# Four graph layers in one kernel: scaling and degree work moved to GpSimd, score halves side by side, loads two groups ahead, tables of their own for both ends, stores from ScalarE

## The chip, the core and the metric

The kernel runs on one core of one Trainium2 chip. The metric is the device time of one execution in microseconds (us), as the median of several executions. A core has a matrix engine (TensorE, PE in the profile; its weight loads are PEld), VectorE (DVE), ScalarE (ACT), GpSimd (POOL) and SyncE (SP), which here issues the DMAs between memory (HBM) and the on-chip SBUF. Each engine runs its own instructions strictly in order and waits on semaphores that others raise. TensorE writes its results to PSUM, eight banks of 2 KB per partition; ScalarE and VectorE read them there.

## What is computed

There are 128 independent samples, each with 128 nodes of 256 features (`x`) and a 128x128 matrix (`adj`). All is float32.

```python
x = ln(x + (adj @ (x @ W0 + b0)) / adj.sum(-1))                       # layer 0
w = mask * INV * sum((x @ Wq) * (adj @ (x * mask) @ Wk), -1)          # layer 1
x = ln(x + softmax(w)[:, None] * (x @ Wv))
s = (q @ k.T) * HD**-0.5 * (adj + adj)    # layer 2: 8 heads of 32, softmax, @ v, @ Wo, + bo
x = ln(x + attention)
H = (adj != 0)                            # layer 3, run twice: W1, relu, layer norm; then W2
out = Dn * (H @ (Be * (H.T @ (x @ W.T)))) + b    # Dn = 1/(H @ adj[0]), Be = 1/H.sum(0)
x = ln(x + out + x)                       # second run of layer 3, and both residuals
```

`ln` is a layer norm over the 256 features without weights.

## The kernel before, in words

Samples are taken in groups of G = 4, so there are 32 groups. A stage is a piece of work for one sample g of a group, such as `ax` (the adjacency times x), `sc0` and `sc1` (the attention scores of the row groups 0, 1 and 2, 3, that is four heads each), `pt` (the eight transposes of the probabilities), `cx` (probabilities times v), `wo`, `tx`, `h1`, `mn`, `y` (layer 3). `ORDER_TEXT` (lines 39 to 79) writes out by hand, for each engine, the order of all stages in one turn of the loop; `sc0.2:3` is stage sc0 of sample 2 into PSUM bank 3 (sc and pt take two banks). A plus marks a stage of the group ahead: one turn does layers 2 and 3 of group q and layers 0 and 1, with the projections `q0 q1 k0 k1` and `v2`, of group q+1. `FIRST` (line 98) is the same table with only the plus stages, run before the loop, and `LAST` (line 99) the table with only the others, run after it; so 31 turns of the whole table lie between. `bank_turns` (line 103) makes TensorE wait until whoever read a bank before has read it.

TensorE's stages are at lines 318 to 448. Most products are done in three passes of the type fp32r (`rows3`, line 337): each matrix is split in a high part, which ScalarE copies out of PSUM (`copy_out`, line 491), and a low part, which VectorE makes by a subtraction (`low`, line 726). The scores (`sc`, line 394) are full float32 products with a contraction of 32 rows: for each of two row groups r, and for each of two column halves c, a product of 32x128 by 32x128.

VectorE multiplies the scores by the adjacency (`sc`, line 821: two instructions of 128x256 for each half, four in a sample), takes their maxima (`zmax`, line 836), computes the statistics of five layer norms (`norm`, line 710), and adds the residuals. Beside that it does the work of each group that belongs to the adjacency: `asum` (line 737, with the copy of the node mask), `am` (line 746, adj transposed times mask), `hold_a` (line 873, a copy of `a_in` that the scores can keep while the next group is loaded), `hyper` (line 791: H, its counts, and H scaled by their reciprocals into `hb`), `dinv` (line 806, four small steps on the degrees), and `x3c_` (line 861, the term of the bias of layer 3, once for each sample).

ScalarE does the exponentials (`attn`, line 561, eight 128x128 in a sample, in place), the copies out of PSUM, and the normalizing step of each norm (`norm`, line 503). GpSimd does the reciprocal root of each norm in three small steps (`root`, line 648), the products of the probabilities (`probs`, line 671, 128x1024) and four kinds of 128x256 additions (`xb_`, `x2c_` and the two of `x3b_`, line 677). SyncE loads x and adj of a whole group with one DMA each (`load_x`, line 277, `load_a`, line 283), for the group that the coming turn reads, and stores one sample at a time (`store`, line 290). In its order the loads stand ahead of the four stores of a turn, so those of the next turn come only after the last store of this one has been issued. `load_a` waits for `a_held`.

```python
            "sp": """ la.0+ lx.0+ store.0 store.1 store.2 store.3 """
            def store(q, g):
                sp.wait_ge(norm_made["ln4"], nth(q, g))
```

## Time and profile before

| what | us |
|---|---|
| median of the 3 runs shown | 1965.06 (1964.87 to 1977.04) |
| the profiled execution's own time | 1963.71 |
| its span, first to last instruction | 1962.0 |
| TensorE (PE) busy | 1873.0 (95%) |
| VectorE (DVE) busy | 1714.7 (87%) |
| ScalarE (ACT) busy | 1478.6 (75%) |
| GpSimd (POOL) busy | 1265.0 (64%) |

The profile is of one execution. Busy times of an engine are shares of the span; the matmuls are pipelined and their ends are modelled, so the start of a block of matmuls and the start of the next one are more exact than the durations between them. In a timeline each row is start, length, engine, line, operation, what it writes and reads, its shapes and how many instructions were merged; what stands in brackets is the idle time of the engine ahead of it and who ended it. A 128x128 float32 product counts as two instructions. The granted clock (PEclk) is 1.00 at TensorE's higher level, 2.4 GHz, and 0.5 at its lower one, 1.2 GHz.

### The profile page before, as it was taken

The numbers are of one execution on the slowest core, as the hardware profiler recorded it, in microseconds if no ns is written. First come the engines' busy times: TensorE is split into PE (matmuls) and PEld (weight loads), VectorE is DVE, ScalarE is ACT, GpSimd is POOL, SyncE is SP. The second block draws the span as 40 slices with busy tenths as digits, with TensorE's granted clock in tenths as the row PEclk, the third lists the DMA queues.
The fourth block names the chain that finished last, engine by engine and source line by source line (L and its number), as shares of the span: only waits on it lengthen the run. The fifth ranks groups of instructions, "written<-read, shape, count | busy, mean of one in ns | idle before, by whom it ended". The sixth has DMA issues, their size and how long they took to land.

```text
span 1962.0 us, 53573 instructions
## 1 busy us (share of the span) xinstructions
PE 1873.0 (95%) x15357; PEld 1630.5 (83%) x15357; DVE 1714.7 (87%) x4867; ACT 1478.6 (75%) x4431; POOL 1265.0 (64%) x2568
## 2 busy tenths in 40 slices
PE   5899999999999999999999999999999999999997
PEld 4788888888888888888888888888888888888886
DVE  5788988888988889888899888889888889888896
ACT  3677778777877777777777878777777778887775
POOL 1466766667765667566667666667666667666665
PEclk9899999999998999899999999999999999999999
DMA  3000000000000000000000000000000000000000
GB/s 112 2 28 28 5 21 27 27 27 27 5 21 27 27 27 21 6 27 27 27 27 7 20 27 27 27 27 8 19 27 27 27 27 5 21 27 27 27 11 12
DMA packets 57546, 46.14 MB, mean 24 GB/s; under 512 B 5168, under 2 KB 56880, under 8 KB 57520
## 3 DMA queue, kind: packets, MB, share of 16 engines
q1 hardware_dynamic: 55760, 43.93, 7.0%
q10 hardware_dynamic: 1760, 1.90, 0.3%
q8 instruction: 12, 0.20, 0.0%
q14 instruction: 14, 0.11, 0.0%
HBM read 29.04 MB, written 16.78 MB: 23 GB/s over the span
## 4 chain that ended last, share of the span: by engine, by line
PE 78%; DMA 5%; issue 5%; DVE 4%; POOL 4%; ACT 2%; SPq 1%; DVEq 0%; POOLq 0%; ACTq 0%
PE ps L340 38%; PE ps L403 7%; PE ps L443 6%; PE ps L411 6%; DMA a_in<-in_adj_dram 4%; PE ps L419 4%; PE ps L324 4%; PE ps L432 4%; PE ps L356 3%; PE ps L392 3%; POOL ln_rs L653 2%; PE ps L350 1%; DVE x2T L732 1%; PE ps L330 1%; ACT y_out L508 1%
## 5 line engine op out<-in xcount | busy, mean ns | idle before, releaser
L564 ACT ACTIVATE z<-z,z_max 128x128 f32<-128x128 f32 x1024 | 399.1, 398 | 7.2 <-DVE z_max L840 3.1
L653 POOL TENSOR_TENSOR ln_rs<-ln_ve,minus_half 128x1 f32<-128x1 f32 x640 | 360.8, 564 | 50.2
L674 POOL TENSOR_TENSOR z<-z,z_rcp 128x1024 f32<-128x1024 f32 x128 | 242.8, 1897 | 192.9 <-DVE z_rcp L847 192.9
L651 POOL TENSOR_TENSOR ln_ve<-ln_mv,eps_col 128x1 f32<-128x1 f32 x640 | 131.1, 205 | 192.7 <-DVE ln_mv L722 192.7
L656 POOL TENSOR_SCALAR ln_nm<-ln_mv,ln_rs 128x1 f32<-128x1 f32 x640 | 179.7, 281 | 109.8 <-POOL ln_rs L653 109.8
L829 DVE SCALAR_TENSOR_TENSOR z<-ps,a_hold 128x256 f32<-128x256 f32 x512 | 190.5, 414 | 61.4 <-PE ps L403 56.7
L340 PE MATMUL ps<-w1T,txT 128*128 128x512 f32 x768 | 205.0, 402 | 1.0 <-DVE txT L732 1.0
L340 PE MATMUL ps<-w2T,mnT 128*128 128x256 f32 x1536 | 202.3, 284 | 0.1
L564 ACT ACTIVATION_READ_ACCUMULATOR z<-z,z_max 128x1 f32 x1024 | 199.7, 195 | 0.0
L340 PEld LDWEIGHTS ps<-w2T,mnT 128*128 128x128 f32 x1536 | 185.6, 189 | 0.3 <-issue 0.3
L840 DVE TENSOR_REDUCE z_max<-z 128x4 f32<-128x512 f32 x256 | 172.3, 673 | 2.2
L664 POOL TENSOR_TENSOR xb<-x_in,b_all 128x256 f32<-128x256 f32 x128 | 92.0, 729 | 121.6 <-DMA x_in<-in_x_dram 111.6
L403 PE MATMUL ps<-kT,qT 32*128 32x128 f32 x2048 | 167.9, 302 | 1.5 <-DVE z L829 0.7
L340 PEld LDWEIGHTS ps<-w1T,txT 128*128 128x128 f32 x768 | 134.7, 188 | 27.8 <-issue 1.2
L403 PEld LDWEIGHTS ps<-kT,qT 32*128 32x128 f32 x2048 | 125.2, 191 | 36.3 <-issue 23.8
L411 PE MATMUL ps<-ident,z 128*128 128x128 f32 x1024 | 134.4, 274 | 11.4 <-issue 9.2
L411 PEld LDWEIGHTS ps<-ident,z 128*128 128x128 f32 x1024 | 115.5, 141 | 26.6 <-issue 22.2
L571 ACT COPY pT<-ps 128x1024 f32<-128x1024 f32 x128 | 129.0, 1008 | 6.2 <-PE ps L411 2.6
L443 PE MATMUL ps<-mp,h 128*128 128x128 f32 x1024 | 132.5, 277 | 0.3 <-issue 0.2
L508 ACT ACTIVATE y_out<-x3b,ln_nm,ln_rs 128x256 f32<-128x256 f32 x128 | 77.3, 604 | 65.5 <-POOL ln_nm L656 65.2
L443 PEld LDWEIGHTS ps<-mp,h 128*128 128x128 f32 x1024 | 122.0, 191 | 4.2 <-issue 0.9
L340 PE MATMUL ps<-w,axT 128*128 128x256 f32 x768 | 125.6, 300 | 0.0
(149 smaller groups left out, 5092.4 us busy)
## 6 DMA issues: line engine op xcount, KB each, us to landing
x_in<-in_x_dram SPq DMA_DIRECT2D x32, 512.0 KB, 4.0
out_dram<-y_out SPq DMA_DIRECT2D x128, 128.0 KB, 1.7
a_in<-in_adj_dram SPq DMA_DIRECT2D x32, 256.0 KB, 2.8
x<-in_L_gnn_Wqk_dram ACTq DMA_DIRECT2D x1, 512.0 KB, 5.6
h<-in_L_gnn_W_dram SPq DMA_DIRECT2D x1, 512.0 KB, 5.3
h<-in_L_gnn_W_dram ACTq DMA_DIRECT2D x1, 512.0 KB, 10.4
v<-in_L_gnn_Wo_dram SPq DMA_DIRECT2D x1, 256.0 KB, 6.2
b_all<-in_L_gnn_b_dram SPq DMA_DIRECT2D x2, 128.0 KB, 8.2
```

The costliest lines, as they stand in the source:

```text
L340: m = pe.matmul(o, left(i, c), right(j, c), start=(k == 0), stop=(k == len(passes) - 1))
L403: m = pe.matmul(ps[:, b + k, c * P:(c + 1) * P], qT[at_, c, g * P:(g + 1) * P], kT[at_, c, g * P:(g + 1) * P], start=True, stop=True)
L411: m = pe.transpose(ps[:, b + h // 4, (h % 4) * P:(h % 4 + 1) * P], z[:, g % 2, h, :], ident[:, :])
L443: m = pe.matmul(o[:, c * P:(c + 1) * P], h1[:, g, c * P:(c + 1) * P], mp[:, g, 0:P], start=True, stop=True)
L564: m = act.activation(z[:, g % 2, h, :], z[:, g % 2, h, :], ACT.Exp, bias=z_max[:, g % 2, h:h + 1], accum_out=z_sum[:, g % 2, h:h + 1])
L571: act.copy(pT[:, g % 2, :, :].rearrange("p (b h) n -> p b (h n)", b=2), ps[:, b:b + 2, :]).then_inc(read["pt"], 1)
L651: pool.tensor_tensor(ve[n][:, g:g + 1], mv[n][:, g, 1:2], eps_col[:, :], ALU.add).then_inc(eps_made[n], 1)
L653: pool.tensor_tensor(rs[n][:, g:g + 1], ve[n][:, g:g + 1], minus_half[:, :], ALU.pow).then_inc(root_made[n], 1)
L656: pool.tensor_scalar(nm[n][:, g:g + 1], mv[n][:, g, 0:1], rs[n][:, g:g + 1], -1.0, ALU.mult, ALU.mult).then_inc(shift_made[n], 1)
L674: pool.tensor_tensor(zg, zg, z_rcp[:, g % 2, :].unsqueeze(2).to_broadcast([P, HEADS, P]), ALU.mult)\
L829: m = dve.scalar_tensor_tensor(out=z[:, g % 2, r * C:(r + 1) * C, :], in0=ps[:, b + k, 0:C * P].rearrange("p (c n) -> p c n", c=C), scalar ...
L840: dve.tensor_reduce(z_max[:, g % 2, hs], z[:, g % 2, hs, :], AX.X, ALU.max, negate=True)\
```

## The change

Nothing is computed differently in substance; the work is spread otherwise.

- The work of a group on the adjacency goes from VectorE to GpSimd: the mask copy, `am` (now one 128x512 product with the mask stretched over the columns, for four of 128x128), `wm`, `hT` (128x512), `hb` (one 128x512 for four 128x128), and most of the degree steps (`dmax` with three small instructions, `dinv` with three). VectorE keeps two reciprocals and a count (`ecnt`, `drcp`); ScalarE copies adj's first column (`hbc`).
- The bias term of layer 3 is made for all four samples at once on GpSimd (`c3_`, two instructions of 128x1024), and `x3b_` is one 128x256 addition in place of two; the `x3c_` of each sample on VectorE goes. For this the last residual carries a factor of one half (`d_half`, half of b2), and ln4 uses a quarter of epsilon.
- `hold_a` goes. A DMA of its own (`load_hold`, twice side by side in SBUF) brings adj again for each sample, and VectorE's score product becomes one 128x512 instruction for each half.
- The scores: in a half the loop over the column halves c is now outside and that over the row groups inside. In the table of the loop three pairs of halves now stand side by side (`sc1.0 sc0.0`, `sc0.1 sc1.2`, `sc0.3 sc1.3`), before it was one.
- x and adj are loaded sample by sample, two groups ahead. The stores are issued by ScalarE, behind its ln4 steps.
- The softmax of layer 1: 1/16 goes into the constant `gram`, the exponential is written in place in PSUM; one small VectorE instruction goes.
- Of what goes, the functions `am`, `hyper`, `dinv`, `sc`, `x3c_` and `hold_a` of VectorE stand in full in the printed kernel above, and the diff shows what comes.
- The order of the loop is a new one for each engine, with `mp.0` and `mp.1` a turn ahead. FIRST and LAST have tables of their own.

```diff
@@ the table of orders @@
 ORDER_TEXT = {
     "pe": """
-        at.0+:3 at.1+:6 at.2+:2 sc0.0:0 mp.0:3 ax.0+:4 ax.1+:5 at.3+:7 sc1.0:2 v2.1:6 sc1.1:0 ax.2+:7
+        at.0+:5 at.1+:3 v2.1:4 sc1.0:0 sc0.0:6 v2.2:2 at.2+:0 ax.0+:3 sc1.1:1 mp.2:5 at.3+:0 ax.1+:3 h0.0+:4
...
     "sp": """
-        la.0+ lx.0+ store.0 store.1 store.2 store.3
+        lh.0+ la.0++ la.1++ la.2++ la.3++ lx.0++ lh.1+ lx.1++ lh.2+ lx.2++ lx.3++ lh.3+
+FIRST_TEXT = {
...
+LAST_TEXT = {
...
-FIRST = {engine: [s for s in schedule if s[2] == 1] for engine, schedule in ORDER.items()}
-LAST = {engine: [s for s in schedule if s[2] == 0] for engine, schedule in ORDER.items()}
+ORDER, FIRST, LAST = ({engine: steps(text) for engine, text in texts.items()}
+                      for texts in (ORDER_TEXT, FIRST_TEXT, LAST_TEXT))
@@ SyncE @@
-                after(sp, made["ax"], q * G)
-                after(sp, xb_made, q * G)
-                sp.dma_start(x_in[:, :, :], x_d[bass.ds(q * G, G)].rearrange("g n d -> n g d")).then_inc(x_loaded, 16)
+                after(sp, made["ax"], before(q, g, G))
+                after(sp, xb_made, before(q, g, G))
+                sp.dma_start(x_in[:, g, :], x_d[bass.ds(q * G + g, 1)].rearrange("g n d -> n (g d)")).then_inc(x_loaded[g], 16)
             def load_a(q, g):
-                after(sp, made["at"], q * G)
+                after(sp, made["at"], before(q, g, G))
                 after(sp, a_summed, q)
-                after(sp, a_held, q)
-                sp.dma_start(a_in[:, :, :], adj_d[bass.ds(q * G, G)].rearrange("g n m -> n g m")).then_inc(a_loaded, 16)
-
-            def store(q, g):
-                sp.wait_ge(norm_made["ln4"], nth(q, g))
-                sp.dma_start(out[bass.ds(q * G + g, 1)].rearrange("g n d -> n (g d)"),
-                             y_out[:, g, :]).then_inc(out_stored[g], 16)
-
-            stages = {"lx": load_x, "la": load_a, "store": store}
+                sp.dma_start(a_in[:, g, :], adj_d[bass.ds(q * G + g, 1)].rearrange("g n m -> n (g m)")).then_inc(a_loaded[g], 16)
+
+            def load_hold(q, g):
+
+                after(sp, read["sc0"], before(q, g, G))
+                after(sp, read["sc1"], before(q, g, G))
+                sp.dma_start(a_hold[:, g, :, :], adj_d[bass.ds(q * G + g, 1)].rearrange("g n m -> n g m").to_broadcast([P, C, P]))\
+                    .then_inc(hold_loaded[g], 16)
...
+            early = [s for s in ORDER["sp"] if s[2] == 2]
+            walk(early, -2)
             walk(FIRST["sp"], -1)
+            walk(early, -1)
             walk(ORDER["sp"], 0)
@@ TensorE @@
-                    if g == 0:
-                        for s in ("q0", "q1", "k0", "k1"):
-                            pe.wait_ge(read[s], q + 1)
-                    for k in range(RG // 2):
-                        r = half * RG // 2 + k
-                        at_ = slice(r * HD, (r + 1) * HD)
-                        for c in range(C):
+                    for s in ("q0", "q1", "k0", "k1"):
+                        pe.wait_ge(read[s], q + 1)
+                    for c in range(C):
+                        for k in range(RG // 2):
+                            r = half * RG // 2 + k
+                            at_ = slice(r * HD, (r + 1) * HD)
                             m = pe.matmul(ps[:, b + k, c * P:(c + 1) * P], qT[at_, c, g * P:(g + 1) * P],
                                           kT[at_, c, g * P:(g + 1) * P], start=True, stop=True)
                     return m
@@ ScalarE @@
+                act.activation(o[0:G, 0:P], o[0:G, 0:P], ACT.Exp, bias=w_stat[0:G, 0:1],
+                               accum_out=w_stat[0:G, 1:2]).then_inc(p_exp_made, 1)
+            def hbc(q, g, o):
+                act.wait_ge(read["at"], nth(q, G - 1))
+                after(act, made["mp"], q * G)
+                act.copy(hb[:, :, P:P + 1], aT[:, :, 0:1]).then_inc(col_made, 1)
+            def store(q, g):
+                act.wait_ge(norm_made["ln4"], nth(q, g))
+                act.dma_start(out[bass.ds(q * G + g, 1)].rearrange("g n d -> n (g d)"),
+                             y_out[:, g, :]).then_inc(out_stored[g], 16)
@@ GpSimd @@
+            def mask_(q, g):
+                after(pool, wm_made, q)
+                after(pool, amT_made, q)
+                pool.tensor_copy(mask[:, :], maskT[:, bass.ds(q * G, G)]).then_inc(mask_made, 1)
+
+            def am(q, g):
+                pool.wait_ge(mask_made, q + 1)
+                pool.wait_ge(read["at"], nth(q, G - 1))
+                after(pool, made["amx"], q * G)
+                pool.tensor_tensor(amT[:, :, :], aT[:, :, :], mask[:, :].unsqueeze(2).to_broadcast([P, G, P]), ALU.mult)\
+                    .then_inc(amT_made, 1)
+
+            def wm_(q, g):
+                pool.wait_ge(mask_made, q + 1)
+                pool.wait_ge(read["xg"], nth(q, G - 1))
+                after(pool, made["wt"], q)
+                pool.tensor_tensor(wm[:, :], w[:, :], mask[:, :], ALU.mult).then_inc(wm_made, 1)
+
+            def hT_(q, g):
+                pool.wait_ge(set_ident, 1)
+                pool.wait_ge(read["at"], nth(q, G - 1))
+                after(pool, made["mp"], q * G)
+                after(pool, cnt_made, q)
+                pool.tensor_scalar(hT[:, :, 0:P], aT[:, :, :], 0.0, 0.0, ALU.is_equal, ALU.is_equal).then_inc(hT_made, 1)
+
+            def hb_(q, g):
+                pool.wait_ge(hT_made, q + 1)
+                pool.wait_ge(ercp_made, q + 1)
+                after(pool, made["mp"], q * G)
+                pool.tensor_tensor(hb[:, :, 0:P], hT[:, :, 0:P], e_rcp[:, :].unsqueeze(2).to_broadcast([P, G, P]), ALU.mult)\
+                    .then_inc(hb_made, 1)
+
+            def dmax(q, g):
+                pool.wait_ge(read["mp"], nth(q, G - 1))
+                pool.tensor_copy(d_sum[:, :], mp[:, :, P]).then_inc(dsum_made, G)
+                pool.wait_ge(set_ident, 1)
+                after(pool, dhalf_made, q)
+                pool.wait_ge(dsum_made, nth(q, G - 1))
+                pool.tensor_scalar(d_max[:, :], d_sum[:, :], TINY, None, ALU.max).then_inc(dmax_made, 1)
+                pool.wait_ge(set_ident, 1)
+                pool.wait_ge(dsum_made, nth(q, G - 1))
+                pool.tensor_scalar(d_pos[:, :], d_sum[:, :], 0.0, 0.5, ALU.is_gt, ALU.mult).then_inc(dpos_made, 1)
+
+            def dinv(q, g):
+                pool.wait_ge(drcp_made, q + 1)
+                pool.wait_ge(dpos_made, q + 1)
+                after(pool, read["y"], q * G)
+                after(pool, dcnt_made, q)
+                pool.tensor_tensor(d_half[:, :], d_pos[:, :], d_rcp[:, :], ALU.mult).then_inc(dhalf_made, 1)
+                pool.wait_ge(dhalf_made, q + 1)
+                after(pool, read["h1"], q * G)
+                pool.tensor_tensor(d_inv[:, :], d_half[:, :], d_half[:, :], ALU.add).then_inc(dinv_made, 1)
+                after(pool, c3_half, q)
+                pool.tensor_tensor(d_cnt[:, :], d_half[:, :], mp[:, :, P + 1], ALU.mult).then_inc(dcnt_made, 1)
+
+            def c3_(q, g):
+                pool.wait_ge(dcnt_made, q + 1)
+                after(pool, x3b_made, q * G)
+                pool.tensor_tensor(c3[:, :, :], bw_all[:, :].unsqueeze(1).to_broadcast([P, G, D]),
+                                   d_cnt[:, :].unsqueeze(2).to_broadcast([P, G, D]), ALU.mult).then_inc(c3_half, 1)
+                pool.wait_ge(c3_half, q + 1)
+                pool.tensor_tensor(c3[:, :, :], c3[:, :, :], b2_all[:, :].unsqueeze(1).to_broadcast([P, G, D]), ALU.add)\
+                    .then_inc(c3_made, 1)
+
             def x3b_(q, g):
                 pool.wait_ge(norm_made["ln2"], nth(q, g))
+                pool.wait_ge(c3_made, q + 1)
                 after(pool, norm_made["ln4"], before(q, g, G))
-                pool.tensor_tensor(x3b[:, g, :], x3[:, g, :], b2_all[:, :], ALU.add).then_inc(x3b_half, 1)
-                pool.wait_ge(x3b_half, nth(q, g))
-                pool.tensor_tensor(x3b[:, g, :], x3b[:, g, :], x3[:, g, :], ALU.add).then_inc(x3b_made, 1)
-
@@ VectorE @@
+            def ecnt(q, g, o):
                 dve.wait_ge(hT_made, q + 1)
+                after(dve, hb_made, q)
                 dve.tensor_reduce(e_cnt[:, :], hT[:, :, :], AX.X, ALU.add).then_inc(cnt_made, 1)
+                dve.wait_ge(cnt_made, q + 1)
+                dve.reciprocal(e_rcp[:, :], e_cnt[:, :]).then_inc(ercp_made, 1)
+
+            def drcp(q, g, o):
+                dve.wait_ge(dmax_made, q + 1)
+                after(dve, dhalf_made, q)
+                dve.reciprocal(d_rcp[:, :], d_max[:, :]).then_inc(drcp_made, 1)
...
+            def z_(half):
+                def run(q, g, o):
                     dve.wait_ge(made[f"sc{half}"], nth(q, g))
-                    dve.wait_ge(a_held, q + 1)
+                    dve.wait_ge(hold_loaded[g], q * 16 + 16)
                     after(dve, made["pt"], before(q, g, 2))
-                    for k in range(RG // 2):
-                        r = half * RG // 2 + k
-                        m = dve.scalar_tensor_tensor(out=z[:, g % 2, r * C:(r + 1) * C, :],
-                                                     in0=ps[:, b + k, 0:C * P].rearrange("p (c n) -> p c n", c=C),
-                                                     scalar=HC, in1=a_hold[:, g, :].unsqueeze(1).to_broadcast([P, C, P]),
-                                                     op0=ALU.mult, op1=ALU.mult)
-                    m.then_inc(read[f"sc{half}"], 1)
+                    b, hs = bank[f"sc{half}", g], slice(half * HEADS // 2, (half + 1) * HEADS // 2)
+                    dve.scalar_tensor_tensor(out=z[:, g % 2, hs, :].rearrange("p (r c) n -> p r (c n)", r=RG // 2),
+                                             in0=ps[:, b:b + RG // 2, 0:C * P], scalar=HC,
+                                             in1=a_hold[:, g, :, :].rearrange("p c n -> p (c n)").unsqueeze(1)
+                                             .to_broadcast([P, RG // 2, C * P]),
+                                             op0=ALU.mult, op1=ALU.mult).then_inc(read[f"sc{half}"], 1)
```

TensorE's order in the loop, from the scores of sample 0 to the transposes `pt.0` (L403 and L475 are the scores, L330 and L402 `at`, L324 and L397 `ax`, L392 and L465 `mp`, L340 and L412 the fp32r products, L411 and L483 `pt`). Before:

```order
L403 MATMUL ps<-kT,qT 128x128 x4
L460 REGISTER_ALU
L403 MATMUL ps<-kT,qT 128x128 x4
L387 REGISTER_ALU
L340 MATMUL ps<-wvT,x2T 128x256 x6
L403 MATMUL ps<-kT,qT 128x128 x4
L460 REGISTER_ALU
L324 MATMUL ps<-aT,x_in 128x128 x2
L403 MATMUL ps<-kT,qT 128x128 x4
L340 MATMUL ps<-w,axT 128x256 x6
```

Now:

```order
L412 MATMUL ps<-wvT,x2T 128x256 x6
L475 MATMUL ps<-kT,qT 128x128 x4
L532 REGISTER_ALU
L475 MATMUL ps<-kT,qT 128x128 x4
L412 MATMUL ps<-wvT,x2T 128x256 x6
...
L475 MATMUL ps<-kT,qT 128x128 x4
L465 MATMUL ps<-hb,hT 128x130
...
L475 MATMUL ps<-kT,qT 128x128 x8
```

Both halves of sample 0 now follow each other with only a register step between, and the two of samples 1 and 2 form a row of x8.

ScalarE's order at the end of a turn (L508 and L580 are the normalizing steps, L533 and L605 the copies of q and k, L656 the stores, L500 and L572 copies). Before:

```order
L508 ACTIVATE y_out<-x3b,ln_nm,ln_rs 128x256 x4
L533 ACTIVATE kT<-ps,bk_col 128x512
L533 ACTIVATE qT<-ps,bq_col 128x512
L641 REGISTER_ALU
L641 COMPARE_AND_BRANCH
```

Now:

```order
L580 ACTIVATE y_out<-x3b,ln_nm,ln_rs 128x256
L572 COPY v<-ps 128x256
L656 ISA
L656 DMA out_dram<-y_out 128x256
L605 ACTIVATE qT<-ps,bq_col 128x512
L580 ACTIVATE y_out<-x3b,ln_nm,ln_rs 128x256
...
L605 ACTIVATE qT<-ps,bq_col 128x512
L580 ACTIVATE y_out<-x3b,ln_nm,ln_rs 128x256
L656 ISA
L656 DMA out_dram<-y_out 128x256
```

The last norm of the turn and its store now stand behind the last copy of q, ahead of everything of the next turn.

## Rows read from the trace of the kernel before

**Rows 1.** The page: busy time of each engine.

```profile
PE 1873.0 (95%) x15357; PEld 1630.5 (83%) x15357; DVE 1714.7 (87%) x4867; ACT 1478.6 (75%) x4431; POOL 1265.0 (64%) x2568
```

**Rows 2.** Timeline of PE: first block of the loop, first block behind it.

```profile
70.11 0.49 PE L330 MATMUL ps<-ident,a_in 128*128 128x128 f32 x3
1907.25 0.72 PE L403 MATMUL ps<-kT,qT 32*128 32x128 f32 x8 [0.31 <-ACT kT L533]
```

**Rows 3.** Busy time by stretches; a turn is about 59 long.

```profile
core 0: us, PE busy (x) PEld busy (x) DVE busy (x) ACT busy (x) POOL busy (x), PEclk, DMA share, GB/s
29.00:70.00 41.00, 28.57 (x148) 22.95 (x148) 21.46 (x71) 13.75 (x34) 15.06 (x34) 0.83 0.06 20
128.00:187.00 59.00, 57.51 (x478) 49.90 (x478) 52.99 (x151) 45.91 (x138) 39.47 (x80) 1.00 0.08 23
187.00:251.00 64.00, 62.06 (x481) 54.13 (x481) 53.55 (x153) 45.92 (x138) 39.54 (x80) 0.92 0.07 23
1907.00:1962.00 55.00, 41.44 (x330) 34.03 (x330) 33.70 (x84) 33.21 (x104) 25.71 (x48) 0.90 0.03 11
```

**Rows 4.** Timeline of PE at the seam of two turns.

```profile
1023.01 0.87 PE L340 MATMUL ps<-wvT,x2T 128*128 128x256 f32 x6
1024.65 0.55 PE L330 MATMUL ps<-ident,a_in 128*128 128x128 f32 x3 [0.77 <-DMA a_in<-in_adj_dram]
1025.20 0.72 PE L403 MATMUL ps<-kT,qT 32*128 32x128 f32 x8
1025.85 0.49 PE L392 MATMUL ps<-hb,hT 128*128 128x130 f32 x2
```

**Rows 5.** Timeline of PE further on in the same turn.

```profile
1034.35 1.04 PE L411 MATMUL ps<-ident,z 128*128 128x128 f32 x8
1035.31 0.72 PE L403 MATMUL ps<-kT,qT 32*128 32x128 f32 x8
1036.34 0.49 PE L392 MATMUL ps<-hb,hT 128*128 128x130 f32 x2 [0.30 <-DVE z L829]
...
1040.27 0.77 PE L403 MATMUL ps<-kT,qT 32*128 32x128 f32 x16
1040.97 0.96 PE L340 MATMUL ps<-w,axT 128*128 128x256 f32 x6
...
1049.07 0.97 PE L340 MATMUL ps<-wvT,x2T 128*128 128x256 f32 x6
1049.88 0.87 PE L340 MATMUL ps<-gram,x1T 128*128 128x256 f32 x6
...
1053.06 1.06 PE L411 MATMUL ps<-ident,z 128*128 128x128 f32 x8 [0.29 <-issue]
1053.88 1.67 PE L340 MATMUL ps<-gram,x1T 128*128 128x256 f32 x12
```

**Rows 6.** Groups of instructions, whole span: busy, mean ns of one, idle before.

```profile
L804 DVE TENSOR_SCALAR hb<-hT,e_rcp 128x128 f32<-128x128 f32 x128 | 87.6, 744 | 1.1
L669 POOL TENSOR_TENSOR x2c<-x,c_all 128x256 f32<-128x256 f32 x128 | 90.2, 736 | 0.0
L674 POOL TENSOR_TENSOR z<-z,z_rcp 128x1024 f32<-128x1024 f32 x128 | 242.8, 1897 | 192.9 <-DVE z_rcp L847 192.9
L656 POOL TENSOR_SCALAR ln_nm<-ln_mv,ln_rs 128x1 f32<-128x1 f32 x640 | 179.7, 281 | 109.8 <-POOL ln_rs L653 109.8
```

**Rows 7.** Timeline of POOL and of DVE from 1020.

```profile
1020.00 2.82 POOL L669 TENSOR_TENSOR x2c<-x,c_all 128x256 f32<-128x256 f32 x4
1020.11 2.80 DVE L804 TENSOR_SCALAR hb<-hT,e_rcp 128x128 f32<-128x128 f32 x4
```

**Rows 8.** One store's issue, and the busier half of ACT's turn.

```profile
1017.03 0.37 SPq L292 DMA_DIRECT2D out_dram<-y_out  x1
...
1025.00:1055.00 30.00, 29.40 (x278) 25.08 (x278) 27.72 (x79) 27.16 (x103) 18.47 (x30) 1.00 0.02 6
```

**Rows 9.** Timeline of the end: the last pt on PE, the last norm on ACT.

```profile
1934.21 1.06 PE L411 MATMUL ps<-ident,z 128*128 128x128 f32 x8 [0.41 <-POOL z L674]
...
1959.20 0.60 ACT L508 ACTIVATE y_out<-x3b,ln_nm,ln_rs 128x256 f32<-128x256 f32 x1 [1.09 <-POOL ln_nm L656]
```

325 lines of the change are left out of this document (172 added, 153 removed).

## The prediction

> **What bounds the kernel now.** I read the page first: PE is busy 95% of the span, DVE 87%, ACT 75%, POOL 64% [rows 1]. Then I cut the span in three by the starts of TensorE's blocks: the setup and FIRST end where the loop's first block starts, at 70.11, and LAST starts at 1907.25 [rows 2]. So 31 turns take 1837.14 us, 59.26 each. The stretches by time say what a turn holds: 57.5 of 59 busy on PE, 53.0 on DVE, 45.9 on ACT, 39.5 on POOL [rows 3]. One stretch, 187 to 251, has the same instructions and takes 62.1 of PE, at a granted clock of 0.92: TensorE ran part of it at 1.2 GHz instead of 2.4, and that cost 62.06 - 57.51 = 4.6 us. Two more turns look like it. Without the three a turn is (1837.1 - 3 x 4.6) / 31 = 58.8 us.
>
> So the loop is TensorE's, and the change can win three things there: waits of PE, work of PE, and the lower clock. The timeline of PE shows the waits. At the seam of two turns the six products of v2 start at 1023.01 and the first `at` at 1024.65, so they hold 1.64 us [rows 4], where six such products take 1049.88 - 1049.07 = 0.81 [rows 5]: 0.83 goes to the wait for `a_in`. A block of scores takes 1025.85 - 1025.20 = 0.65 [rows 4]; the one at 1035.31 takes 1.03 up to the next block, because `mp` waits for VectorE to read the bank: 0.38. Before the `pt` at 1053.06 stand 0.29 idle [rows 5].
>
> The scores themselves are a find. A half alone (x8) takes 0.65 us, and the one place where both halves stand together (x16) takes 1040.97 - 1040.27 = 0.70 [rows 5]: four row groups run beside each other, so the second half is nearly free. A lone half also costs something on the way in: eight transposes take 1035.31 - 1034.35 = 0.96 when scores follow and 1053.88 - 1053.06 = 0.82 when others do, 0.14 more [rows 5].
>
> **The change part by part, for one turn.**
> Scores. Three pairs in place of one: two halves fewer stand alone. Each saves 0.65 + 0.65 + 2 x 0.14 - 0.70 - 0.14 = 0.74, two save 1.48; I take 1.4, as one of the pairs may find a bank unread. That c is now the outer loop moves nothing in a pair, where the row groups overlap already. The work of all other products is the same; their new order changes who follows whom, by 0.1 or so at a place, of either sign, and I take zero (bounds: 0.8 saved, 0.5 lost).
> Loads. `a_in` of the next group now is asked for right after its `at` of this turn and lands a turn early, and the stores no longer stand ahead of it in SP's queue. The 0.83 goes. SP issues 12 loads in a turn, each about as long as a store's issue, 0.37 [rows 8], with waits between that end early; 12 x 0.37 = 4.4 of some 56, nothing on the path.
> Waits for a bank and before `pt`: 0.38 + 0.29 go in the main, with the new order and a faster VectorE.
> VectorE. It loses `hb`, `am`, the hold copy, `x3c` and a dozen small steps. The trace says how much `hb` really cost: four 128x128 products take 2.80 us, in step with four additions of GpSimd, 2.82 [rows 7]. Neither engine's operation is that long by its size (744 ns for 128 columns of hb [rows 6]), so these two held each other up, and the move ends it. VectorE goes from 53 to well under 48 of a turn. It is not the bound, so this is worth only what the waits above are.
> GpSimd. Its additions of 256 columns take 736 ns, its product of 1024 columns 1897 [rows 6]: 1.51 ns a column and 0.35 to start. A 128x512 then is 0.35 + 512 x 0.00151 = 1.12 us. New: `am` 1.12, `hb` 1.12, `hT` (one input; no row shows it; between a tiny step, 0.28 [rows 6], and 1.12; I take 0.8, nearer the wide one), the two of `c3` 3.8, nine small steps of 0.2 to 0.28, 2.1. Gone: four of the eight additions of x3b, 2.9. Net 6.0, so 39.5 + 6.0 = 45.5 of 56. That is below PE's bound, but in order: `c3.0` stands ahead of `ln3_root.0`, `am.0` ahead of `probs.0`.
> ACT. Four stores of 0.37 and their register steps, together 2.0 to 2.4; `hbc` 0.1. Net 45.9 + 2.3 = 48.2 of 56. In its busy half it is 27.2 of 30 already [rows 8], and the last norm and store now stand ahead of the next turn's copies of `at` and `ax`. If everything else is in place this costs nothing; the bound above is a wait of 1.5 a turn at the seam. I take zero, because TensorE has two `v2` and two score halves to do there that need no copy of `at`.
> Sum of a turn: 58.8 - 1.4 - 0.83 - 0.38 - 0.29 = 55.9 us; bounds 55.0 (the order saves 0.8 more) and 57.4 (ACT's 1.5).
> The lower clock. It came in turns that have the 0.8 idle at the seam. With less idleness I keep one such turn of three, 4.6; bounds 0 and 10.
> FIRST. 41.0 us, PE busy 28.6 [rows 3]: a chain of latencies through norms, with new order but the same steps, and `mp` added. I take 1 less (bounds 3 less, 1 more).
> LAST. 54.8 from 1907.25 to 1962.0. The last `pt` starts at 1934.21, 27.0 after the start, and from there the chain of sample 3 takes to the last norm at 1959.20 + 0.60, and the store [rows 9]. That tail is one sample's chain and stays, 27.8. What the new table can do is bring the four samples' exponentials together at the front: ACT's 33.2 us of work in LAST [rows 3] is more than half exponentials. I take the last `pt` at 22.5, so 4.5 less (bounds 1 and 8).
> Sum: 70.1 - 1.0 + 31 x 55.9 + 4.6 + 54.8 - 4.5 = 1856.9 us of span. The profiled execution's own time is 1.7 above its span, and the median of the three runs 1.35 above that: 1860.
>
> **The rivals.**
> (A) PE packed. All new order fits, no low clock: 55.0 a turn, LAST 8 less. 69.1 + 1705 + 46.8 + 3 = 1824. For it: PE waits are few and each has a cause that the change touches. Against: ACT's 90% in half a turn.
> (B) ACT takes over. ln4_norm.3 needs the root on GpSimd, the store waits for the norm, and behind it stand `v2.1`, `at.0`, `at.1`, then `ax`; TensorE stops at `ax` or at `pt.0`. Price 1.0 to 1.5 a turn: 1860 + 31 x 1.3 = 1900. For it: ACT waits for ln_nm at the seam now, and the copies of `at` already come straight behind. Against: TensorE has two of `v2` and both score halves in between.
> (C) The pairs save nothing, say because each half waits for its bank, and the 1.4 stay: 1860 + 31 x 1.4 = 1903. Against it stands the measured x16.
> (D) Slower: GpSimd becomes the bound. It works in order, and `am`, `hT`, `hb` and `c3` put 6.8 us of wide work ahead of the norm's roots and the probabilities, on which TensorE waits through ACT. It has 10.5 us of room in a turn, so it decides once the wide operations take over (6.8 + 10.5) / 6.8 = 2.5 times my price. At 3.5 times a turn is 45.5 + 17 = 62.5, and the time 1860 + 31 x 6.6 = 2065. For it: no row shows a product with an operand stretched over columns in `am`'s form or a one-input `hT`. Against: the 1897 ns of z is just such a product with z_rcp stretched.
> The Trainium skill, page GPSIMD Engine Reference, section Engine selection, speaks against moving this work: it says in its table to do elementwise work on VectorE, GpSimd being about 2x slower for two inputs. By that and the trace's 744 ns (which the lockstep inflates) four `hb` would come to 6 us, and the turn of GpSimd to about 51, still under 56; the trace's 736 ns for 256 columns points lower.
>
> **How the numbers follow.** Forecast 0.60, A 0.14, B 0.16, C 0.05, D 0.05. The time is the forecast's, 1860. Its own bounds are 1835 to 1890. The range has to hold eight in ten: half of A and nearly all of B come in, so 1826 to 1902. A measurement of this kernel can tell about 1% from no change. Forecast, A, B and C are all more than 3% faster; D is slower, but a mild D can end within 1%: faster 0.94, same 0.02, slower 0.04.
>
> **What would show it right or wrong.** Right: turns of 55 to 57 us; the score rows on PE three x16 in a turn at 0.70 each; the idle time of `at` behind a DMA gone; DVE under 48 of a turn and POOL at 44 to 47; fewer turns with a clock of 0.92; the last `pt` about 22 into LAST. Wrong: PE idle with ACT copies of `at`, `ax` or `pt` as the releaser (B), x8 rows at 0.65 where the table has pairs (C), `c3`, `am` or `hb` above 2.5 us with roots late behind them (D), or a period near 58.8 although the named waits are gone, which would say that TensorE's blocks cost more in the new order than in the old.

## The result, and the profile after

| | before | after |
|---|---|---|
| median, us | 1971.05 (4 runs, 1964.87 to 1986.92) | 1892.68 (4 runs, 1891.20 to 1894.28) |
| the profiled execution: own time, span | 1963.71, 1962.0 | 1894.28, 1892.6 |
| setup and FIRST, up to the loop | 70.1 | 64.7 |
| a turn (31) | 59.26 | 57.34 |
| LAST | 54.8 | 50.4 |

The ratio to the kernel before is 0.959, 95% interval 0.953 to 0.966: 4% faster, inside the range, 33 us behind the forecast of 1860. The page of the changed kernel, the line that answers to [rows 1]:

```profile
PE 1824.7 (96%) x15357; PEld 1607.5 (85%) x15357; DVE 1448.7 (77%) x3909; ACT 1449.6 (77%) x4463; POOL 1438.7 (76%) x2857
```

VectorE is down by 266 us and GpSimd up by 174. TensorE, which bounds the loop, has lost only 48. By stretches (answers to [rows 3]): setup's end and FIRST, one turn, the whole loop, LAST; the columns are as there.

```profile
30.00:65.00 35.00, 28.46 (x155) 23.53 (x155) 17.59 (x55) 14.33 (x38) 20.03 (x41) 0.85 0.09 24
...
1038.00:1095.00 57.00, 55.85 (x478) 49.31 (x477) 44.33 (x122) 44.98 (x139) 44.85 (x89) 1.00 0.11 32
...
64.70:1842.20 1777.50, 1742.39 (x14820) 1538.59 (x14819) 1386.19 (x3749) 1394.88 (x4309) 1386.22 (x2752) 1.00 0.10 32
1842.20:1892.60 50.40, 38.23 (x326) 32.42 (x326) 30.98 (x69) 32.69 (x102) 29.34 (x55) 0.92 0.04 14
```

In the loop TensorE is busy 1742.4 of 1777.5, so 35 us, 1.1 a turn, are idle. The list of waits of the changed kernel (in all, times, longest) says where:

```profile
PE ps L397 <- ACT aT L572: 22.4, 30, 0.8
PE ps L465 <- DVE z L950: 7.6, 31, 0.2
```

The wait for `a_in` of [rows 4] is gone, and a new one has come at nearly the same place: `ax.0` now waits for ScalarE's copy of `aT`. The timeline there, the chain from the last stats of the turn on; ACTq is ScalarE issuing a DMA:

```profile
1038.11 0.18 DVE L874 BATCH_NORM_AGGREGATE ln_mv<-ln_st 128x2 f32<-128x6 f32 x1
...
1038.37 0.19 POOL L736 TENSOR_TENSOR ln_ve<-ln_mv,eps_col 128x1 f32<-128x1 f32 x1 [2.36 <-DVE ln_mv L874]
...
1039.36 0.26 POOL L741 TENSOR_SCALAR ln_nm<-ln_mv,ln_rs 128x1 f32<-128x1 f32 x1 [0.17 <-POOL ln_rs L738]
1039.65 0.60 ACT L580 ACTIVATE y_out<-x3b,ln_nm,ln_rs 128x256 f32<-128x256 f32 x1 [0.54 <-POOL ln_nm L741]
...
1040.41 0.34 ACTq L656 DMA_DIRECT2D out_dram<-y_out  x1
...
1041.28 0.37 ACT L572 COPY v<-ps 128x256 f32<-128x256 f32 x1 [1.03 <-issue]
1041.59 0.56 ACT L572 COPY aT<-ps 128x128 f32<-128x128 f32 x2
1042.05 0.38 ACT L572 COPY v<-ps 128x256 f32<-128x256 f32 x1
1042.28 0.71 PE L397 MATMUL ps<-aT,x_in 128*128 128x128 f32 x4 [0.77 <-ACT aT L572]
```

From the start of the norm to the first copy are 1.63 us. In between stands one store: it waits for the norm to end, is issued in 0.34, and its register steps follow; the profile books most of that as idle, because issuing is not counted as busy. The scores, the other place on which the forecast rested (answers to [rows 5]):

```profile
1039.32 1.17 PE L475 MATMUL ps<-kT,qT 32*128 32x128 f32 x16
...
1040.42 0.98 PE L412 MATMUL ps<-wvT,x2T 128*128 128x256 f32 x6
...
1045.31 1.08 PE L475 MATMUL ps<-kT,qT 32*128 32x128 f32 x16
```

A pair takes 1.10 here, not 0.70: 0.455 to the start of the second half, then 0.64. The second pair takes 1.01, the third 0.67. The line of the waits on the q and k copies (L470) has 24 semaphore rows in a turn on TensorE's sequencer, where the kernel before had 5: the change dropped the condition `if g == 0`, so the four waits stand ahead of every half. This was in the diff, and the forecast passed over it. The view of the order ("only a register step between") shows no semaphore waits.

The third pair has the same waits and does not suffer. First the rows of L470 and the pair at the first place, then those of the third pair, in one turn:

```profile
L470 PEldq EVENT_SEMAPHORE  x5: 51/51/1492, 923.0 to 925.0; - x5
924.67 1.17 PE L475 MATMUL ps<-kT,qT 32*128 32x128 f32 x16
...
L470 PEldq EVENT_SEMAPHORE  x6: 51/51/51, 939.5 to 940.0; - x6
939.68 1.03 PE L483 MATMUL ps<-ident,z 128*128 128x128 f32 x8
940.65 0.74 PE L475 MATMUL ps<-kT,qT 32*128 32x128 f32 x16
```

At the first place the waits run up to 925.0, between the products of the pair. At the third they are over by 940.05, while the eight transposes ahead of the pair are still at work, and the pair starts at 940.65.

For the whole turn I added up TensorE's blocks by kind, from the first product of a block to that of the next, each a median over the turns of the loop (us a turn). The last three columns are kernels of the next section; the one with the loads ahead of the stores is the kernel before with that edit, the other two are the changed kernel with one edit.

| blocks | before | after | waits once | loads ahead of stores | stores on SyncE |
|---|---|---|---|---|---|
| sc0 + sc1 | 4.99 | 4.39 | 3.94 | 4.99 | 4.39 |
| at | 0.75 | 1.28 | 1.50 | 0.63 | 0.35 |
| v2 | 4.08 | 3.37 | 3.37 | 3.15 | 3.37 |
| mp | 1.60 | 1.03 | 1.03 | 1.32 | 1.03 |
| amx | 2.36 | 1.69 | 1.70 | 2.35 | 1.70 |
| ax | 2.14 | 1.98 | 2.22 | 2.07 | 1.96 |
| pt + cx | 5.84 | 6.27 | 6.28 | 5.84 | 6.26 |
| all | 58.83 | 57.38 | 57.40 | 57.41 | 56.43 |

The kinds not in the table are in "all": 37.1 before, 37.4 in the changed kernel. The idle time ahead of a block counts to the block before it.

### The profile page after: what moved, and what is told of

It is laid out like the page before. It is cut to its first block, busy times and chain, and to the rows that moved or that the text cites. A ratio compares the mean times of both kernels' runs of the same rounds, so it can differ in the third digit from the quotient of the medians.

```text
span 1892.6 us, 54990 instructions
## 1 busy us (share of the span) xinstructions
PE 1824.7 (96%) x15357; PEld 1607.5 (85%) x15357; DVE 1448.7 (77%) x3909; ACT 1449.6 (77%) x4463; POOL 1438.7 (76%) x2857
## 4 chain that ended last, share of the span: by engine, by line
PE 87%; DVE 4%; issue 3%; ACT 2%; POOL 2%; ACTq 1%; SPq 0%; DMA 0%; DVEq 0%; POOLq 0%
PE ps L412 50%; PE ps L515 6%; PE ps L483 6%; PE ps L475 4%; PE ps L491 4%; PE ps L397 4%; PE ps L428 3%; PE ps L504 3%; PE ps L465 2%; PE ps L449 2%; PE ps L422 2%; DVE z L950 1%; ACT y_out L580 1%; POOL ln_rs L738 1%; DVE ln_st L869 1%
## 5 line engine op out<-in xcount | busy, mean ns | idle before, releaser
L738 POOL TENSOR_TENSOR ln_rs<-ln_ve,minus_half 128x1 f32<-128x1 f32 x640 | 351.8, 550 | 50.2
L741 POOL TENSOR_SCALAR ln_nm<-ln_mv,ln_rs 128x1 f32<-128x1 f32 x640 | 169.2, 264 | 109.8 <-POOL ln_rs L738 109.8
L580 ACT ACTIVATE h<-h,ln_nm,ln_rs 128x512 f32<-128x512 f32 x128 | 104.5, 817 | 143.3 <-POOL ln_nm L741 140.8
L736 POOL TENSOR_TENSOR ln_ve<-ln_mv,eps_col 128x1 f32<-128x1 f32 x640 | 121.8, 190 | 118.5 <-DVE ln_mv L874 118.3
L412 PE MATMUL ps<-w1T,txT 128*128 128x512 f32 x768 | 208.9, 407 | 1.1 <-DVE txT L884 1.0
L412 PE MATMUL ps<-w2T,mnT 128*128 128x256 f32 x1536 | 204.4, 282 | 0.0
L950 DVE SCALAR_TENSOR_TENSOR z<-ps,a_hold 128x512 f32<-128x512 f32 x256 | 174.1, 681 | 37.9 <-PE ps L475 34.3
L412 PEld LDWEIGHTS ps<-w2T,mnT 128*128 128x128 f32 x1536 | 191.9, 188 | 9.0 <-issue 0.2
L412 PEld LDWEIGHTS ps<-w1T,txT 128*128 128x128 f32 x768 | 137.2, 188 | 29.4 <-DVE txT L884 1.9
L986 DVE SCALAR_TENSOR_TENSOR x3b<-ps,d_half,x3b 128x256 f32<-128x256 f32 x128 | 60.9, 475 | 116.2 <-PE ps L412 115.1
L475 PE MATMUL ps<-kT,qT 32*128 32x128 f32 x2048 | 142.4, 295 | 2.2 <-ACT qT L605 0.9
L475 PEld LDWEIGHTS ps<-kT,qT 32*128 32x128 f32 x2048 | 112.5, 185 | 28.4 <-issue 16.6
L874 DVE BATCH_NORM_AGGREGATE ln_mv<-ln_st 128x2 f32<-128x6 f32 x640 | 111.6, 174 | 25.7 <-DVE ln_st L869 0.5
L483 PE MATMUL ps<-ident,z 128*128 128x128 f32 x1024 | 129.5, 275 | 1.6 <-POOL z L758 1.5
L884 DVE TENSOR_TENSOR mnT<-ps,mnT 128x512 fp32r<-128x512 f32 x128 | 88.1, 688 | 53.9 <-ACT mnT L572 50.5
```

What stands on the lines that cost most here:

```text
L412: m = pe.matmul(o, left(i, c), right(j, c), start=(k == 0), stop=(k == len(passes) - 1))
L475: m = pe.matmul(ps[:, b + k, c * P:(c + 1) * P], qT[at_, c, g * P:(g + 1) * P], kT[at_, c, g * P:(g + 1) * P], start=True, stop=True)
L483: m = pe.transpose(ps[:, b + h // 4, (h % 4) * P:(h % 4 + 1) * P], z[:, g % 2, h, :], ident[:, :])
L580: act.activation(dst(g), src(g), ACT.Identity, bias=nm[n][:, g:g + 1], scale=rs[n][:, g:g + 1]).then_inc(norm_made[n], 1)
L738: pool.tensor_tensor(rs[n][:, g:g + 1], ve[n][:, g:g + 1], minus_half[:, :], ALU.pow).then_inc(root_made[n], 1)
L741: pool.tensor_scalar(nm[n][:, g:g + 1], mv[n][:, g, 0:1], rs[n][:, g:g + 1], -1.0, ALU.mult, ALU.mult).then_inc(shift_made[n], 1)
```

## The experiments

Times are medians of 4 runs. The kernel before gave 1963 to 2013 in these runs, so a ratio to it is loose by 0.6%; the other kernels keep within 0.2% and are compared by their own times.

**Waits once.** Theory: the surplus waits lengthen the pairs.

```diff
-                    for s in ("q0", "q1", "k0", "k1"):
-                        pe.wait_ge(read[s], q + 1)
+                    if g == 0 and half == 1:
+                        for s in ("q0", "q1", "k0", "k1"):
+                            pe.wait_ge(read[s], q + 1)
```

> The changed kernel with the waits on the q and k copies only ahead of the first score half of a turn (in the changed kernel they stand ahead of all eight halves: 24 semaphore rows at L470 a turn). Theory (these waits stand in TensorE's sequencer between the halves of a pair and cost its matmuls time): the adjacent pairs that take 1.10 and 1.01 us come down to about the 0.67 of the third pair, 0.43 + 0.34 = 0.77 us a turn, over 31 turns -24 us: about 1869. Rival (what a pair gives is waited for again at the end of the turn, where TensorE waits for the aT copy 0.77 us): the pairs fall and the wait at L397 grows by as much: within 5 us of the changed kernel's 1893. Second rival (the waits cost nothing, the second half is slow for its operands): pairs unchanged, 1893.

Measured: 1893.04 (1891.81 to 1895.01), the same as the changed kernel. The pairs did shrink, to 0.89 and 0.78, not to the 0.67 of the third pair, and all of it came back. What keeps the first two above the third is open. Its rows at the seam, and its first line of waits:

```profile
1036.89 0.96 PE L476 MATMUL ps<-kT,qT 32*128 32x128 f32 x16
1039.85 0.71 PE L397 MATMUL ps<-aT,x_in 128*128 128x128 f32 x4 [0.94 <-ACT aT L573]
```
```profile
PE ps L397 <- ACT aT L573: 27.8, 30, 1.0
```

Of the 0.45 us a turn that the scores gave up, 0.22 went to `at` (the wait for aT) and 0.24 to `ax.3`, ahead of the first `pt`. The second place the rival had not named. TensorE does not set the pace at these two places: making the pairs shorter returned nothing.

**Stores on SyncE.** The same four stores, issued by SyncE at the end of its turn, behind the loads.

```diff
     "act": """
...
-        v2.0+ store.0 q1.0+ ln4_norm.1 k1.0+ store.1 mp.1+ ln4_norm.2 k0.0+ store.2 q0.0+ ln4_norm.3 store.3
+        v2.0+ q1.0+ ln4_norm.1 k1.0+ mp.1+ ln4_norm.2 k0.0+ q0.0+ ln4_norm.3
     "sp": """
...
+        store.0 store.1 store.2 store.3
```

> The changed kernel with the four output stores issued by SyncE behind its loads of the turn, ScalarE free of them; all else the same. Theory (two or more store issues of 0.34 us stand in the chain from the last stats to the aT copies of the next turn, where TensorE waits 0.77 us at L397): the wait falls by 0.34 to 0.77 us a turn, 11 to 24 us in all: 1869 to 1882. Rival (the chain stats, aggr, root, norm holds ScalarE, the store only fills a gap in it): the wait stays at 0.6 to 0.8 and the time at 1893. Second rival (the stores on SyncE hold up the loads again as before): TensorE waits for a_in, and the time is above 1893.

Measured: 1865.31 (1864.73 to 1865.93), 28 us less than the kernel with the waits once, on the same chip. A turn is 0.91 shorter by its starts (57.34 to 56.42), more than my upper bound of 0.77: the idle row books 0.77, but the block `at.2` shrank by 0.93, from 1.04 to 0.11. The wait at L397 is gone from the list. And my theory counted two or more issues in the chain; there is one. ScalarE, same place:

```profile
1023.38 0.60 ACT L586 ACTIVATE y_out<-x3b,ln_nm,ln_rs 128x256 f32<-128x256 f32 x1 [0.52 <-POOL ln_nm L747]
1023.89 0.37 ACT L578 COPY v<-ps 128x256 f32<-128x256 f32 x1
...
1024.19 0.56 ACT L578 COPY aT<-ps 128x128 f32<-128x128 f32 x2
...
1025.10 0.66 PE L403 MATMUL ps<-aT,x_in 128*128 128x128 f32 x4
```

The copy now starts 0.51 after the norm's start, where it took 1.63: one store costs the chain 1.12, three times its row of 0.34. `ax.0` finds its aT ready.

**Place or load?** Does the place of the store cost, or ScalarE's load? Here ScalarE keeps all its stores, and only the last norm and the last store move behind the first copies of the next turn, where it waits for the second `v2` anyway (a minus marks a step of the turn before; LAST has the same move, and the loop of ScalarE begins one turn later).

```diff
-        v2.1 at.0+ at.1+ v2.2 at.2+ ax.0+ exp1.0
+        v2.1 at.0+ at.1+ ln4_norm.3- store.3- v2.2 at.2+ ax.0+ exp1.0
...
-        mp.1+ ln4_norm.2 k0.0+ store.2 q0.0+ ln4_norm.3 store.3
+        mp.1+ ln4_norm.2 k0.0+ store.2 q0.0+
```

> The changed kernel, its stores still issued by ScalarE, but the last layer norm of a turn and the last store stand in ScalarE's next turn behind its first three copies (v2.1 and the two aT), where ScalarE waited for the second v product anyway; its second turn is written out like the first (the loop begins at the third). Theory from the two runs before (TensorE waits at L397 for the ScalarE chain last stats, aggr, root, norm, store, three copies; it is the place of the norm and the store in that order that costs, not ScalarE's total work): the wait at L397 goes from 0.75 us a turn to under 0.1 and the time to about that of the kernel with stores on SyncE, 1863 to 1870. Rival (ScalarE is simply too full with the stores, what is moved comes up again before the exponentials): the wait moves to the score or pt steps and the time stays above 1880.

Measured: 1866.47 (1864.38 to 1867.74). ScalarE does as much work as in the changed kernel, and all but a microsecond of the gain is there. So it was the place of these two steps, not ScalarE's 77%.

**Both, and both with the norm moved.** The first kernel has the waits once and the stores on SyncE, the second has the moved norm as well.

> Both edits: waits on q and k once, stores by SyncE. If both theories hold and the two are separate: -24 and -11 to -24, some 1845 to 1858. If one takes back what the other gives (TensorE earlier at the seam finds ScalarE late), the sum is short: 1865 to 1880.

> The kernel with both edits (waits on q and k once, stores by SyncE), with the last norm moved in the same way. There the q and k waits gave back 0.41 us a turn at two places: 0.17 at L403 for the aT copy, and 0.24 ahead of the first pt, for the probabilities on GpSimd (1.90 us). Theory: the first goes and the second stays, or shrinks as the exponentials begin earlier: 0.17 to 0.41 us a turn, 5 to 13 us under 1864: 1851 to 1859. Rival (the whole chain up to the exponentials is set by VectorE's row maxima, not by the copies): 1862 to 1866.

Measured: 1864.32 (1863.06 to 1865.41) and 1865.40 (1864.23 to 1867.24). Neither beats the 1865.31 by more than the spread, and my theory of 5 to 13 us more from the moved norm failed: four kernels end at 56.4 to 56.5 us a turn. In the last of them the first `pt` starts 9.22 us after the first scores (1024.09 to 1033.31), as it does without the move (1022.60 to 1031.82). The rows in between, of the kernel with everything:

```profile
1025.03 0.69 DVE L960 SCALAR_TENSOR_TENSOR z<-ps,a_hold 128x512 f32<-128x512 f32 x1 [0.56 <-PE ps L482]
...
1025.79 0.32 PE L408 MATMUL ps<-ident,a_in 128*128 128x128 f32 x1
...
1026.07 0.71 PE L403 MATMUL ps<-aT,x_in 128*128 128x128 f32 x4
...
1026.81 0.37 ACT L579 CAST axT<-ps 128x256 fp32r<-128x256 f32 x1 [0.19 <-PE ps L403]
...
1027.08 0.40 ACT L648 ACTIVATE z<-z,z_max 128x128 f32<-128x128 f32 x1
...
1031.00 0.18 DVE L978 RECIPROCAL z_rcp<-z_sum 128x8 f32<-128x8 f32 x1
...
1031.26 1.90 POOL L768 TENSOR_TENSOR z<-z,z_rcp 128x1024 f32<-128x1024 f32 x1 [1.10 <-DVE z_rcp L978]
...
1033.28 0.86 PEld L490 LDWEIGHTS ps<-ident,z 128*128 128x128 f32 x8 [0.29 <-issue]
```

I read these rows so: VectorE frees the bank of `at.2` (bank 0) at 1025.72, then come `ax.0`, its copy, eight exponentials among other copies, the reciprocal and GpSimd's 1.90, and TensorE has waited. My theory for this run had the aT copy as the end of the wait ahead of `ax.0`. But the block `at.2` stayed at 0.28 with the copy moved ahead (0.11 with the stores on SyncE alone), so it is not the copy; that the late bank is the cause is read from the rows. No run touched this chain, so that it is the next bound is argued, not shown.

**Product order in a half.** The waits once, and the c loop inside the row groups as before.

> The waits once, and inside a half the c loop inside the row groups as before the change. Theory: the change of product order does nothing for the time of a half, so it is within 6 us of the run with the waits once, half and pair durations within 0.03 us. Rival (the order of the products lets neighbouring row groups overlap): a half grows by 0.1 us, eight a turn, and the time by 25 us.

Measured: 1891.72 (1891.36 to 1893.28), pairs of 0.89 and 0.78. The time is the same within the spread, so the order of the products does nothing.

**Halves apart.**

```diff
-        sc1.0:0 sc0.0:6 v2.2:2 at.2+:0
+        sc1.0:0 v2.2:2 sc0.0:6 at.2+:0
...
-        sc0.1:0 sc1.2:5 ax.2+:4
+        sc0.1:0 ax.2+:4 sc1.2:5
```

> The changed kernel with two of its three score pairs taken apart: v2.2 between sc1.0 and sc0.0, ax.2 between sc0.1 and sc1.2. Theory (what pays in a pair is that the halves stand behind one another): apart each half takes about 0.65 us, so 1.30 for 1.10 and 1.30 for 1.01, 0.20 + 0.29 = 0.49 us a turn more of TensorE. Of this the 0.77 us that TensorE waits for the aT copy hides the first 0.20; the second is paid: +9 us, about 1902; +15 (1908) if nothing is hidden, as the later second half delays VectorE too. Rival (the seam's wait takes both up): within 3 us of 1893.

Measured: 1909.97 (1909.02 to 1910.96), +17, beyond the +15 of my worst case, though the wait at L397 fell from 22.4 to 12.4 us. The halves took 0.644 alone, and `sc0.1` 0.776. The scores grew by 0.59 a turn, and the turn by 0.54, though `at` gave back 0.28. So taking pairs apart costs time. Whether it is the longer blocks, or that a half which comes late lengthens the chain to the first `pt`, the run does not part.

**hT back on VectorE** (one instruction ahead of its count, the rest as changed).

> The changed kernel with the not-equal count of the whole adjacency (hT, 128x512) back on VectorE as one operation ahead of ecnt, GpSimd free of its 1.94 us. Theory (GpSimd at 76% has room, nothing TensorE waits for hangs on hT): within 4 us of 1893. Rival (GpSimd's queue delays the probabilities and the roots by that operation, and TensorE waits for them): faster by up to 1.1 us a turn, down to 1860. Other side: VectorE is 0.3 us late in the middle of the turn and TensorE waits for it: up to +10 us.

Measured: 1907.46 (1906.64 to 1908.37), +15, above my +10 for the other side. VectorE needs 610 ns for what takes GpSimd 1941:

```profile
L928 DVE TENSOR_SCALAR hT<-aT 128x512 f32<-128x512 f32 x32 | 19.5, 610 | 0.0
```
```profile
PE ps L428 <- DVE h L975: 10.2, 31, 0.4
```

The short step on the busier path costs TensorE 0.33 us a turn of idle time at that one wait; the block ahead of it, `xg.2`, grew by 0.49, which is the whole growth of a turn. The list of waits of the changed kernel has nothing at this place.

**The old ends.** FIRST and LAST filtered from the new loop order, as before the change.

> The changed kernel with the first and last turn filtered from the loop's order, as before the change, not by tables of their own. Theory: the first turn before the loop goes back from 34.5 us to about 40.9 and the last from 50.4 to about 54.8: +6 and +4 us, about 1903. Rival (the gains at the ends came from the shorter loop order and the early loads, not from the tables): within 3 us of 1893.

Measured: 1906.11 (1905.20 to 1908.20), +13. The loop starts 38.6 us after the setup for 34.5, and LAST takes 60.9 for 50.4 (the filtered order is even worse than before's 54.8). So the tables of their own are worth about 13 us, more than I gave.

**Loads one group ahead** (stores still on ScalarE).

> The changed kernel, its loads (still one per sample, on SyncE, the stores on ScalarE) only one group ahead, in the order adjacency, x, held adjacency. Theory (what held the loads of the kernel before was the stores that stood ahead of them in SyncE's queue; without these one group ahead is early enough): within 4 us of 1893 and no wait of TensorE for a_in. Rival (the second group ahead is what hides the landing of 1.9 to 2.2 us): TensorE waits for a_in again, up to 0.8 us a turn, 1893 to 1918.

Measured: 1894.08 (1893.53 to 1895.25), and no wait of TensorE for `a_in`. The second group ahead does nothing.

**The kernel before, with one part each.** First the stores on ScalarE alone; then all on SyncE, with only the loads ahead of the stores (the second plus lets them go out in the turn before, once the adjacency has been copied).

```diff
-        la.0+ lx.0+ store.0 store.1 store.2 store.3
+        la.0+ lx.0+                                    # stores on ScalarE, behind its last norms
+        la.0++ lx.0++ store.0 store.1 store.2 store.3  # the other kernel
```

> The kernel before with one part of the change alone: the four stores issued by ScalarE behind its last norms, SyncE left with the loads. Theory: TensorE's wait for a_in (0.83 us a turn) goes, and the issues of 0.34 us stand in ScalarE's chain to the aT copies of the next turn, which gives back 0.3 to 0.7 of it: 0 to -16 us against the kernel before, some 1955 to 1975. Rival (ScalarE's issues cost nothing here): -26 us, about 1945. Second rival (they cost more than the wait did): slower than before.

> The kernel before with its two loads of the next group ahead of the four stores in SyncE's queue (all still on SyncE; the loads are written one group further ahead, so they go out as soon as VectorE has copied the adjacency). Nothing else of the change. Theory (the rest of the change gives almost nothing in the loop; what pays is that the loads no longer stand behind stores that wait for the last norm, and the stores on ScalarE cost the kernel before little): about the time of the kernel before with stores on ScalarE, 0.963 of before, or up to 10 us below it. Against the changed kernel with stores on SyncE (1865), which has the rest of the change as well, it then stands 40 to 50 us longer: that is what the rest is worth once ScalarE's stores are out of the way. Rival (ScalarE's stores cost here what they cost in the changed kernel, 0.9 us a turn): 0.949 of before, and the rest is worth 15 to 20 us. Second rival (the stores, now behind the loads, hold up y_out or the loads as before): 0.98 to 1.0 of before.

Measured: 1914.51 (1913.23 to 1915.07), ratio 0.963 (0.958 to 0.967); and 1906.76 (1905.35 to 1908.29), ratio 0.960 (0.955 to 0.965). Both are far beyond the first's theory of 0 to -16 us. The kernel before ran slower beside these two (medians 1990 and 1983) than beside the change (1971), so their ratios look as good as its 0.959; by their own times the second stands 14 us behind the change. The order of one queue does most of what the whole change does. Its seam, in place of [rows 4]:

```profile
1103.12 0.87 PE L343 MATMUL ps<-wvT,x2T 128*128 128x256 f32 x6
1103.83 0.49 PE L333 MATMUL ps<-ident,a_in 128*128 128x128 f32 x3
1104.26 0.72 PE L406 MATMUL ps<-kT,qT 32*128 32x128 f32 x8
```

The six `v2` products hold 0.71 where they held 1.64. `mp` gave another 0.28, `at` 0.12 and `ax` 0.07, so the loads brought 1.4 a turn where the wait's own row says 0.83. Here is the account of the loop. A turn goes from 58.8 (without the turns at the lower clock) to 57.4 by the loads alone; to 56.4 by the rest of the change, if the stores are SyncE's; and back to 57.3 because ScalarE issues them. In the old order ScalarE's stores cost less: 57.65 a turn for the 57.42 with all on SyncE. In span, 1904.7 of the second against 1892.6 of the change are 12.1 us, of which the two ends are 9.7 and the 31 turns 2.5.

## Why the prediction was right or wrong

- **The range.** The measured 1892.68 lies outside the forecast's own bounds (1835 to 1890). The range held it because rival B was let in, and B's 1900 kept the full gain of the pairs, which did not come: the number is near partly by luck.
- **Loads (-0.83).** Right: the block shrank from 1.62 to 0.80 (medians), and to 0.71 in the kernel that has the loads ahead alone. That nothing of it needs two groups was not foreseen, and not that the loads alone bring 1.4 a turn.
- **Scores (-1.4 taken).** Failed in size: 4.99 to 4.39, so -0.60. The step that failed is the 0.74 that each pair saves: it took the x16 of [rows 5] as the price of any pair and left out the waits that the diff puts between the halves. Without them it is -1.05, still short of the 1.4. And the 0.45 between the two gave no time here. (The text says that two halves fewer stand alone; it is two pairs, four halves, and the sum counts it so.) Rival C (the pairs save nothing) was half right in the block. In time it was wrong as it stands: two pairs taken apart cost 17 us.
- **ScalarE at the seam (0 taken).** Failed: it costs 0.91 a turn, 28 us. The reason given, "TensorE has two `v2` and two score halves to do there that need no copy of `at`", compared TensorE's work ahead of `ax` with the copies alone. The chain that has to fit beside it is longer: the statistics, the root, the norm, a store and three copies, from 1038.11 to the end of the second aT at 1042.15. Rival B had the mechanism and the place, with 1.0 to 1.5 a turn somewhat dear.
- **`mp`'s bank and the idle ahead of `pt` (-0.38, -0.29).** Right in the main. `mp` blocks fell by 0.57, half of it by the loads alone, but 0.25 a turn still waits at L465, for VectorE's z. The idle time ahead of `pt.3` stood behind `amx.3`: that block fell from 0.89 to 0.41, so the 0.29 is in the 0.67 that `amx` gave. The rest of that, and the 0.43 by which `pt` and `cx` grew, stood under the zero for the new order.
- **The lower clock (one turn kept, 4.6).** The clock of the loop is 1.00 throughout, and so it is in all the twelve kernels of the runs. The turns at 0.92 also went away in the two kernels that differ from the one before in their stores and loads alone: they came with the wait for `a_in`. But the changed kernel waits 0.8 us near the same place, for ScalarE, and keeps the clock, so that the wait by itself was the cause is not shown.
- **FIRST (-1.0).** Too small: the loop starts 5.4 earlier, though the setup ended 1 later. **LAST (-4.5).** Measured -4.4; its last `pt` starts at 1865.34, 23.1 into it, for 22.5.
- **GpSimd and VectorE.** GpSimd is busy 44.9 in a turn of 57 for the 45.5, so rival D was far off; VectorE's 44.3 is under the 48. In GpSimd's terms errors of both signs met: `hT` 1941 ns for the 0.8 us, the two of `c3` 4.3 for 3.8, `am` and `hb` 1.04 for 1.12, and the sixty small steps of the norms' roots in a turn are some 15 ns shorter each (ln_nm 264 for the 281 of [rows 6]), which makes 0.9. (Four `hb` at 744 ns would have made GpSimd's turn 50.3 by the prediction's own terms, not 51; nothing hangs on it.)

```profile
L822 POOL TENSOR_TENSOR c<-c,b_all 128x1024 f32<-128x1024 f32 x32 | 76.9, 2403 | 2.5
...
L784 POOL TENSOR_SCALAR hT<-aT 128x512 f32<-128x512 f32 x32 | 62.1, 1941 | 0.0
L819 POOL TENSOR_TENSOR c<-bw_all,d_cnt 128x1024 f32<-128x1024 f32 x32 | 60.6, 1893 | 0.0
...
L790 POOL TENSOR_TENSOR hb<-hT,e_rcp 128x512 f32<-128x512 f32 x32 | 33.3, 1041 | 0.6 <-DVE e_rcp L937 0.6
```

The sum closes: 1856.9 predicted, FIRST -4.4, the turns +1.44 x 31 = +44.6, the lower clock -4.6, LAST +0.1, makes 1892.6, the span. Of the 1.44, 0.80 are the scores and 0.91 the stores of ScalarE; the other kinds take the difference back.

The best version is the change with the stores back on SyncE, behind its loads: 1865, 1.5% under the change; its ratio to the kernel before is 0.944 (0.938 to 0.951).

## What to carry over

A store that waits for the end of a chain must not stand ahead of a load in one queue. But the queue it is moved to has to be one whose next step nobody waits for: a store's row of 0.34 us cost 1.12 in the chain in which it stood. When the bound engine has slack at a seam, add up the whole chain that must fit beside it, not its last step. And in a diff look for conditions that vanish: waits already satisfied still take time on a sequencer, where no earlier work of the engine hides them.
